# Second-order attention: the output's two state products as 32x32 tiles beside U and W, in the state's PSUM bank, copied out by VectorE

## What is computed

```python
def step(carry, qkv):
    S_K, C_QV, G = carry
    q_t, k_t, v_t = qkv
    C_prev = GAMMA * C_QV
    k_C = jnp.einsum('bhk,bhkv->bhv', k_t, C_prev)
    G = GAMMA * G + k_t[..., :, None] * k_C[..., None, :]
    S_K = GAMMA * S_K + k_t[..., :, None] * k_t[..., None, :]
    C_QV = C_prev + q_t[..., :, None] * v_t[..., None, :]
    S_C = jnp.einsum('bhij,bhjv->bhiv', S_K, C_QV)
    o_t = jnp.einsum('bhk,bhkv->bhv', q_t, S_C - G)
    return ((S_K, C_QV, G), o_t)
```

## Time and profile before

| | us |
|---|---|
| median of 3 runs | 3567.26 (3558.9 to 3573.87) |
| the profiled execution | span 3568.7 |
| of it, the visits of this stage | about 1516 to 2755 |
| TensorE busy over the span | 3320.9 (93%) |
| VectorE, ScalarE, GpSimd busy | 2210.7, 2104.6, 1505.5 |

### The profile page before, as it was taken

How to read it: one execution, slowest core, us unless ns; L and a number is a source line. 1 busy time by engine, 2 the same in 40 slices (tenths; PEclk the granted TensorE clock), 3 DMA queues, 4 the chain that set the end, 5 groups by cost and what they waited for, 6 DMA issues and landing times. The chain is left out here.

```text
span 3568.7 us, 133004 instructions
## 1 busy us (share of the span) xinstructions
PE 3320.9 (93%) x52918; PEld 2939.5 (82%) x52918; DVE 2210.7 (62%) x6377; ACT 2104.6 (59%) x6626; POOL 1505.5 (42%) x2318
## 2 busy tenths in 40 slices
PE   8939999799956999899999999999998999999998
PEld 8939999777746999888888888888887888888877
DVE  6675555678775555555544444444444788888887
ACT  5555655455445555444444444444443699999996
POOL 5754655300014665343434434343443633333225
PEclk9969999999977999999999999999999999999998
DMA  4143433612144343500000000000000143333333
GB/s 130 49 154 94 95 90 64 164 32 65 52 138 128 89 96 75 151 3 3 3 3 3 3 3 3 3 3 3 3 3 17 37 123 113 117 113 101 105 97 100
DMA packets 203003, 235.05 MB, mean 66 GB/s; under 512 B 18064, under 2 KB 183072, under 8 KB 202400
## 3 DMA queue, kind: packets, MB, share of 16 engines
q1 hardware_dynamic: 177824, 192.99, 17.1%
q0 software_dynamic: 24576, 33.57, 5.6%
HBM read 147.46 MB, written 79.04 MB: 63 GB/s over the span
## 5 line engine op out<-in xcount | busy, mean ns | idle before, releaser
L2513 ACT ACTIVATE wa_S<-wa_S,wa_top 128x192 f32<-128x192 f32 x1024 | 462.9, 476 | 36.6 <-DVE wa_top L2609 36.6
L1965 DVE TENSOR_TENSOR so_raw<-so_rows,so_masks 128x1024 f32<-128x1024 f32 x256 | 313.6, 1225 | 227.2 <-PE so_rows L1655 218.3
L2609 DVE CUSTOM_DVE_ANT_0 wa_S<-wa_bank,wa_band 128x192 f32<-128x192 f32 x1024 | 295.3, 350 | 3.4 <-issue 3.4
L2045 POOL TENSOR_TENSOR so_spread<-so_state,so_head 128x256 f32<-128x256 f32 x224 | 137.4, 613 | 339.3 <-PE so_bankC L1743 307.9
L1956 DVE SCALAR_TENSOR_TENSOR so_state<-so_state,so_bankX 128x96 f32<-128x96 f32 x192 | 48.8, 254 | 347.4 <-PE so_bankX L1780 347.4
L2050 POOL TENSOR_TENSOR so_OT<-so_O,so_OT 128x128 fp32r<-128x128 f32 x256 | 116.9, 457 | 343.2 <-ACT so_OT L1884 343.2
L1878 ACT COPY so_O<-so_bankC 128x128 f32<-128x128 f32 x256 | 68.4, 267 | 320.7 <-PE so_bankC L1743 320.6
L650 POOL DMA_INDIRECT sum_dram<-y,rows x128 | 224.1, 1750 | 29.4 <-issue 27.2
L2401 PE MATMUL wa_bank<-ident,wa_S 128*128 128x128 f32 x1536 | 222.0, 277 | 7.7 <-ACT wa_probT L2520 4.7
L2513 ACT ACTIVATION_READ_ACCUMULATOR wa_S<-wa_S,wa_top 128x1 f32 x1024 | 223.7, 218 | 0.0
L728 ACT ACTIVATE m2e_hT<-m_bank,m2e_bias 128x256 fp32r<-128x256 f32 x256 | 126.4, 494 | 150.5 <-PE m_bank L680 144.5
(11 more groups left out here) (457 smaller groups left out, 9991.9 us busy)
## 6 DMA issues: line engine op xcount, KB each, us to landing
m_w_raw<-in_L_ffn_W_dram SPq DMA_DIRECT2D x64, 512.0 KB, 3.7
wa_V<-wa_V_dram SPq DMA_DIRECT2D x256, 128.0 KB, 2.8
sum_dram<-X SPq DMA_DIRECT2D x16, 1024.0 KB, 4.7
X<-sum_dram SPq DMA_DIRECT2D x16, 1024.0 KB, 8.2
wa_V_dram<-wa_V_new SPq DMA_DIRECT2D x32, 512.0 KB, 3.5
wa_V_rest<-wa_V_dram SPq DMA_DIRECT2D x128, 128.0 KB, 3.0
X<-in_L_attn_a_x_dram SPq DMA_DIRECT2D x8, 1024.0 KB, 11.2
xn_dram<-m2r_xn SPq DMA_DIRECT2D x16, 512.0 KB, 4.5
```

The source lines that it names most:

```text
L1965: nc.vector.tensor_tensor(AB[:, t % 2].rearrange("p h m t -> p h (m t)"), rows4[:, :, 0:2 * P], masks[:].rearrange("p m t -> p (m t)")[:, ...
L2045: nc.gpsimd.tensor_tensor(whole[:, t % UT], new[:, :, None, :].broadcast_to([P, 2, HG, DK]), head[:, None, :, None].broadcast_to([P, 2, HG ...
L2513: nc.scalar.activation(S[:, n % 2, z], S[:, n % 2, z], ACT.Exp, bias=top[:, n % 2, z:z + 1], scale=-1.0, accum_out=sums[:, i % 2, SET * c ...
L2609: nc.vector.tensor_tensor_reduce(out=S[:, n % 2, z], in0=bS[g][:, eo * SPAN:(eo + 1) * SPAN], in1=band[:], scale=-(D ** -0.5), scalar=3e38 ...
```

## The change

The output's state products go from two full products to eight 32x32 ones and are done in visit t for t-1, right behind those into U and W; they open the accumulation, and values_to_O closes it. Head h of the output uses array tile (h, h+2), so its rows in PSUM are those of head h+2 (crossed_rows), and Wo is loaded with its rows crossed alike, by four DMAs. The output moves from bankC to bankX columns 352 to 479. VectorE copies it out (copy_O), ahead of the state's update. so_spread, the head mask and spread_state are gone, and so are the semaphores O_done and state_spread. TensorE waits between state_to_UW and state_to_O for O_copied, S_ready and x_ready, where it waited for O_copied ahead of state_to_UW and for S_ready and x_ready ahead of state_products. At in_pair 2 mix comes ahead of turn_x.

```diff
-        spread = sb("spread", [P, UT * 2 * HG * DK])
-        wo_raw = spread[:, 0:UT * HID].rearrange("p (u d) -> p u d", u=UT)
+        wo_raw = sb("wo_raw", [P, UT, HID])
...
+        O_AT = slice(HID + 3 * DK, HID + 3 * DK + P)
...
+        def crossed_rows(h):
+            return head_rows((h + 2) % HG)
...
-                sp.dma_start(wo_raw, A["L1_attn_a_Wo"].rearrange("(u p) d -> p u d", p=P)).then_inc(s_["o_loaded"], 16)
+                wo_rows = A["L1_attn_a_Wo"].rearrange("(u p) d -> p u d", p=P)
+                for h in range(HG):
+                    sp.dma_start(wo_raw[crossed_rows(h)], wo_rows[head_rows(h)]).then_inc(s_["o_loaded"], 16)
...
                 def mix(i, t):
                     pe.wait_ge(s_["O_ready"], UT * (i + 1))
                     pe.wait_ge(s_["S_ready"], updates_to(min(t - 2, NU - 1)))
+                    pe.wait_ge(s_["O_copied"], min(t - 1, NU))
...
                 def state_to_O(t):
                     pe.wait_ge(s_["Ug_ready"], carries_to(t))
-                    pe.wait_ge(s_["WT_ready"], min(t + 2, NU))
-                    pe.wait_ge(s_["state_spread"], updates_to(t - UT))
-                    nc.tensor.matmul(bC[:, P:2 * P], whole_of(t, 2), Ug[:, t % 2], start=False, stop=False)
-                    nc.tensor.matmul(bC[:, P:2 * P], whole_of(t, 1), QTg[:, tile(t) % 2, t % UT], start=False, stop=True
-                                     ).then_inc(s_["O_done"], 1)
+                    for h in range(HG):
+                        nc.tensor.matmul(bX[crossed_rows(h), O_AT], state_of(t, 2, h), Ug[head_rows(h), t % 2],
+                                         start=True, stop=False, tile_position=(h * DK, (h + 2) % HG * DK))
+                    for h in range(HG):
+                        nc.tensor.matmul(bX[crossed_rows(h), O_AT], state_of(t, 1, h), QTg[head_rows(h), tile(t) % 2, t % UT],
+                                         start=False, stop=False, tile_position=(h * DK, (h + 2) % HG * DK))
...
                 def state_products(t):
-                    if t >= 1:
-                        pe.wait_ge(s_["S_ready"], updates_to(t - 1))
-                    if mixes_to(t + 1) >= 1:
-                        pe.wait_ge(s_["x_ready"], mixes_to(t + 1))
...
-                    if 2 <= t < NU + 2 and carries(t - 2):
-                        state_to_O(t - 2)
...
+                    for m in mixes_at(t):
+                        mix(m, t)
                     if in_pair == 2 and p + 1 < NT // 2:
                         turn_x(p + 1)
-                    for m in mixes_at(t):
-                        mix(m, t)
...
-                    if 2 <= t < NU + 2:
-                        pe.wait_ge(s_["O_copied"], t - 1)
...
                     if t < NU and carries(t):
                         state_to_UW(t)
+                    if 2 <= t <= NU:
+                        pe.wait_ge(s_["O_copied"], t - 1)
+                        pe.wait_ge(s_["S_ready"], updates_to(t - 2))
+                        if mixes_to(t) >= 1:
+                            pe.wait_ge(s_["x_ready"], mixes_to(t))
+                    if 1 <= t <= NU and carries(t - 1):
+                        state_to_O(t - 1)
...
+                def copy_O(t):
+                    dve.wait_ge(s_["C_done"], t + 2)
+                    dve.wait_ge(s_["S_done"], updates_to(t))
+                    if t >= UT:
+                        dve.wait_ge(s_["O_ready"], t - UT + 1)
+                    nc.vector.tensor_copy(O[:, t % UT], bX[:, O_AT]).then_inc(s_["O_copied"], 1)
...
                 for t in range(NU + 4):
+                    if 2 <= t < NU + 2:
+                        copy_O(t - 2)
                     if 2 <= t < NU + 2 and updates(t - 2):
                         update(t - 2)
```

## The result

The changed kernel takes 3632.07 us (median of 4 runs, 3628.07 to 3637.42), the kernel before 3568.19 us on the same chip (4 runs, 3558.9 to 3573.87): a ratio of 1.0178, 95% interval 1.0165 to 1.0191. It is slower by 64 us. The direction and the long waits were as forecast, and the time lies inside the whole range of 3560 to 3636. The size was not as forecast: I had put the loss at 26 us and the likely times at 3580 to 3612.

A forecast was written before the change was run, and what follows sets the result against it. TensorE's instruction stream was taken to bound the stage; -109.8 (removed products) + 58.8 (output's block) + 19.8 + 57 (waits) = +25.8 us, giving 3593 us; forecast's own range 3580 to 3612, whole range 3560 to 3636.

The forecast's parts named there:

- I take 0.25: TensorE's block of state products: the output's four chained passes per tile lengthen it by 0.25 us in 216 visits.
- Rival 1: Output's tiles don't run beside U's and W's, sharing their rows: 0.43 us instead of 0.25, 39 us more, 3632; chance 0.13.
- The wait of in_pair 2: TensorE waits before the output's products for the residual, behind low_xT and turn_x: 1.9 us in 30 visits, 57 us.
- The wait of in_pair 7: TensorE waits before the output's products for the residual after the mix: 0.6 us in 33 visits, 19.8 us.
- No visit has slack on TensorE: Waits added to TensorE's stream in the stage are paid in full, since nothing gives them back.
- priced at 0.60: Eight visits with the output's products but without U and W pay the block anew, 0.38 + 0.22 = 0.60 us each.
- rival 2: Output's passes hide in TensorE's 0.20 us gap, costing 0 to 0.05 us: -19 to -29 us, about 3545; chance 0.08.
- rival 3: TensorE's waits cost only some 60 us and the output's block 0.20: +0 to +10 us, about 3573; chance 0.17.
- The removed products: Output's two full 128x128 state products leave TensorE in 224 visits, 0.49 us each: 109.8 us saved.
- rival 4: TensorE's long waits bring its clock down: half a visit at half speed, 30 times, about 60 us more, 3650; chance 0.05.
- VectorE's copy of the output: The added 128x128 PSUM copy takes some 0.29 us in a 0.59 us idle stretch ahead of the mask: costs nothing.
- Wo's four DMAs: In the prologue, Wo loads as four DMAs instead of one while VectorE idles: costs nothing, at worst a few us.

The follow-up runs named there:

- e1: Changed kernel with the output's four waits (O_copied, S_ready, x_ready, Ug_ready) moved ahead of U's products; 3654.53 us, ratio 1.0237.
- e7: Changed kernel with residual ahead of low_xT and the output's waits ahead of U's products, except x_ready in visits with a mix; 3550.54 us, ratio 0.995.
- e2: Changed kernel with VectorE's residual ahead of low_xT; 3593.72 us, ratio 1.0057.
- e3: Changed kernel with turn_x ahead of mix again, as in the kernel before; 3603.46 us, ratio 1.0089.
- e8: As e7, but mixes of even tiles write bankJ in place of bankX, and V's projection waits for x_ready; 3518.64 us, ratio 0.9858.

## Why the prediction was right, and where it was wrong

The stage, from its first visit to its last, grew from 1230.6 to 1292.9 us, by 62.3; my sum said 25.8. By position in the pair, forecast from my own terms against measured:

| in_pair | 0 and 1 | 2 | 3 | 4 | 5 | 6 | 7 | sum |
|---|---|---|---|---|---|---|---|---|
| forecast | -14.6 | +51.8 | -5.8 | -5.8 | -3.8 | -7.7 | +11.5 | +25.8 |
| measured | -15.4 | +52.7 | +2.6 | +1.2 | +4.5 | -0.4 | +17.1 | +62.3 |

54 of the 62 us are differences of medians, 8 are irregular long visits; a further 4 lie ahead of the stage.

- **The step that failed: "I take 0.25" for the output's block.** It measured 0.43 in ordinary visits (0.81 - 0.38), 0.18 more in each: that is the whole gap at in_pair 3 to 6, apart from irregular visits. By the sum's own count of 216 visits that is 39 us. The count of passes was right, as e1 and e7 show with 0.24. Missing was what the change writes between the blocks: four waits, compiled into two wait instructions that TensorE's queue works off one by one, 0.11 us apart, while the 32x32 products ahead of them are too short to cover it. I had asked of each wait only whether its event was long over, found that it was, and priced it at nothing. The kernel before already held a hint: in the earlier trace rows an empty queue needs 0.31 us from release to product, and I used that figure only for the long waits.
- **Rival 1 named the right number for a wrong reason, which is luck.** It gave 0.43 and 3632. Its mechanism, tiles that share rows exclude each other, is refuted by e1 and e7, in which U, W and the output start within 0.05 us. Of the rule that speaks for it (the Trainium skill, "TensorE: Matmul & The Clock Gate", Part 3: weight loads overlap running products only in other row groups) those rows show no trace.
- **The wait of in_pair 2** was forecast as 1.9 us in visits that grow by about 1.7: U to O measured 2.00, visits grew by 1.71. e2 and e3 show its cause by undoing it.
- **The wait of in_pair 7** was forecast as 0.6 us from 0.06 behind U: by the same count it measured 0.73 (0.79 - 0.06), and the visits grew by 0.50 instead of 0.36. The 0.6 had 0.13 us for the release, which measured 0.26 with wait instructions to work off and 0.05 without. e8 shows that the shared bank is the cause of the wait.
- **"No visit has slack on TensorE" was wrong for in_pair 0.** There ScalarE's copy of V was late in the kernel before, and TensorE waited for it ahead of W's product: 30 times in the stage, 8.9 us; in after once, 0.6 us. The first line is of before, t = 40, the others are from the lists of waits of before and after:

```profile
1708.14 0.16 PEld L1756 LDWEIGHTS so_bankC<-so_raw,so_V 128*32 128x32 f32 x8 [0.21 <-ACT so_V L1859]
...
PEld so_bankC L1756 <- ACT so_V L1859: 8.9, 30, 0.6
...
PEld so_bankC L1759 <- ACT so_V L1861: 0.6, 1, 0.6
```

So part of the late start runs under a wait that was there before: these visits fall by 0.24 us (4.98 to 4.74), and in the seven whose output block was priced at 0.60 although U and W have none, the fall is 0.46 where my terms gave a rise of 0.11. In_pair 1 has no such cover and falls by 0.06 instead of 0.24. The column "0 and 1" agrees with the forecast because the two misses cancel, 5.1 us one way at in_pair 0 and 3.9 the other at in_pair 1.
- **Two side sums were slightly off**: by its own terms rival 2 gives -28 to -17 instead of -29 to -19, and rival 3 with waits of 60 us gives -2 instead of 0. Neither touches the forecast.
- **The removed products** are worth 0.49 us a visit: with e7's block (+0.24) an ordinary visit is 4.60, and 4.83 - 0.49 + 0.24 = 4.58.
- **The clock** stayed at 1.00 in the stage with idle stretches of 1.55 us, so rival 4 did not come. VectorE's copy of the output takes 0.292 us (0.29 forecast) and costs nothing that I can find:

```profile
L1956 DVE COPY so_O<-so_bankX 128x128 f32<-128x128 f32 x256 | 74.7, 292 | 507.3 <-PE so_bankX L1769 449.7
```

- **Wo's four DMAs**: after starts its stage 4.0 us later than before, but the other seven kernels have the same four DMAs and start between 1.4 us earlier and 2.5 us later. So I count the DMAs as nothing that these runs can tell; what the 4.0 us are stays open.

Open: the irregular long visits. In e2, for example, the visits t = 141 to 154 are mostly 1.0 to 1.4 us over their kind's median, at a granted clock of 1.00 and with idle stretches on TensorE. Counted as what visits more than 0.15 us over their kind's median have too much, they come to 13 us in before (19 visits), 20 in after, 34 in e2, 22 in e7 and 12 in e8: the kernel before has them too. Part of them (5 of the 19 in before, 17 of 45 in e2) hold one gap of 0.76 to 1.26 us in the weight path, among the products of keys and queries or of queries with U, that nothing in the profile ended. The first line is of before, t = 80, the second of e2, t = 148:

```profile
1899.34 0.30 PEld L1655 LDWEIGHTS so_rows<-so_U,so_QT 32*128 32x128 f32 x4 [0.76 <-issue]
...
2249.81 0.19 PEld L1651 LDWEIGHTS so_rows<-so_KT,so_QT 32*128 32x128 f32 x2 [0.83 <-issue]
```

No run was made for them, and their cause isn't known.

## What to carry to other kernels

A wait whose event is long past is not free: count the wait instructions that will stand between two short products on TensorE, and put waits ahead of a long block, or leave only one, which rides on the product. When two steps of one engine are swapped, follow what each of them feeds into the *queues* of the others: here the cheap step (residual) became late because it stood behind another (low_xT) that the swap had moved back. When a result moves into a bank that others use, look at who fills that bank last ahead of it; another bank was worth 32 us in e8, of which the medians explain 16.

## What the runs showed of the hardware that I had not expected

- On TensorE each wait instruction for a count already reached cost about 0.11 us between 32x32 blocks (U to O 0.128, 0.239, 0.345 us with one, two and three), the first only 0.075, and nothing behind a block of long products (U starts 2.79 us into the visit with or without two more of them ahead).
- Three sets of 32x32 tiles that share their rows pairwise, of which each set writes one bank through four row tiles, run side by side, each set into four different quarters of its bank's rows: starts at 2049.05, 2049.08 and 2049.10 in e7. The Trainium skill, "TensorEngine Tiling (Array Packing)", "Restrictions and Gotchas", excludes that for row tiles in one bank; these rows disagree.
